# A Mamba and mixture-of-experts block on one core: the accumulating transfers of blocks 6 and 7 are sent first as a pair, those of blocks 0 to 5 after them

## The reference, cut to what matters

```python
x = L0_attn_x
xn = _layernorm(x, axis=-1)
x = x + _L0_attn_ref(xn, ...) + _L0_ffn_ref(xn, ...)
```

```python
top_logits, sel = jax.lax.top_k(logits, TOP_K)          # TOP_K = 2
probs = jax.nn.softmax(top_logits, axis=-1)
h = silu(einsum('td,edh->eth', xt, w1)) * einsum('td,edh->eth', xt, w3)
y = einsum('eth,ehd->etd', h, w2)
out = einsum('ktd,tk->td', y[sel.T, t_idx], probs)
```

## Time and profile before

| | us |
|---|---|
| median of 3 runs | 491.26 (490.94 to 491.74) |
| the profiled execution, whole time | 491.12 |
| its span, first to last instruction | 489.1 |
| DVE busy | 410.9 (84%) |
| PE busy | 436.3 (89%) |
| POOL busy | 319.8 (65%) |
| DMA queue of POOL | 25.52 MB, 19.6% of 16 engines' span |
| DMA queue of SP | 35.37 MB, 28.3% |

### The profile page before, as it was taken

The page is one execution under the profiler, slowest core; times in us unless marked ns, Lnnn a source line. Parts: engine busy times, 40 slices in busy tenths (PEclk is TensorE's granted clock), DMA queues, the critical chain, the costliest instruction groups (busy, mean ns, idle before and its releaser), DMA issues. The chain is left out here.

```text
span 489.1 us, 8269 instructions
## 1 busy us (share of the span) xinstructions
PE 436.3 (89%) x2188; PEld 318.8 (65%) x2188; DVE 410.9 (84%) x868; ACT 311.5 (64%) x421; POOL 319.8 (65%) x345
## 2 busy tenths in 40 slices
PE   0989959899999999998999999999999999996853
PEld 0887525555555555553788989888888999543432
DVE  5999986999999999996996777767776886894995
ACT  2775657888898888988544444343444555797650
POOL 3647778777787777680177777777777777755110
PEclk9999989999999999999999999999999999999975
DMA  9601139121121212132668776666665651049994
GB/s 246 176 3 46 56 105 168 52 75 63 50 87 49 89 45 84 39 114 57 175 190 231 225 210 181 193 184 180 176 183 160 184 170 60 7 79 204 211 194 129
DMA packets 70939, 62.75 MB, mean 128 GB/s; under 512 B 9034, under 2 KB 63214, under 8 KB 70912
## 3 DMA queue, kind: packets, MB, share of 16 engines
q1 hardware_dynamic: 57728, 35.37, 28.3%
q0 software_dynamic: 10944, 25.52, 19.6%
q10 hardware_dynamic: 2240, 1.57, 1.0%
HBM read 38.94 MB, written 29.64 MB: 140 GB/s over the span
## 5 line engine op out<-in xcount | busy, mean ns | idle before, releaser
L572 POOL DMA_INDIRECT moe_out<-xnT,dst_u x142 | 145.5, 1024 | 64.3 <-issue 31.7
L558 POOL DMA_INDIRECT moe_in<-xn,slot_u x128 | 141.6, 1106 | 46.1 <-issue 35.7
L1092 ACT ACTIVATE xn<-PA 128x1024 f32<-128x1024 f32 (+1 forms) x36 | 36.6, 1017 | 61.3 <-PE PA L803 52.7
L1447 DVE TENSOR_TENSOR xn<-xn,PB 128x1024 f32<-128x1024 f32 (+1 forms) x36 | 43.4, 1206 | 33.2 <-PE PB L803 29.2
L837 PE MATMUL PD<-xnT,xn 128*128 128x128 f32 x536 | 65.7, 275 | 0.0
L837 PEld LDWEIGHTS PD<-xnT,xn 128*128 128x128 f32 x536 | 62.8, 192 | 0.0
L1307 DVE SCALAR_TENSOR_TENSOR acc<-PA,cw,acc 128x255 f32<-128x255 f32 (+2 forms) x96 | 54.3, 607 | 8.2 <-ACT acc L1001 8.0
L685 PE MATMUL PC<-xc,Wc 128*128 128x512 f32 x128 | 57.7, 593 | 1.8 <-ACT xc L1048 1.8
L658 PE MATMUL PD<-xc,WgB 128*128 128x512 f32 x128 | 58.5, 601 | 0.0
L658 PEld LDWEIGHTS PD<-xc,WgB 128*128 128x128 f32 x128 | 24.8, 195 | 31.3 <-issue 31.3
L672 PE MATMUL PB<-WoT,y 128*128 128x128 f32 x240 | 32.2, 290 | 13.2 <-DVE y L1283 13.2
(11 more groups left out here) (211 smaller groups left out, 936.0 us busy)
## 6 DMA issues: line engine op xcount, KB each, us to landing
xnT<-in_L_ffn_w_dram SPq DMA_DIRECT2D x108, 128.0 KB, 2.3
xn<-moe_in SPq DMA_DIRECT2D x31, 266.0 KB
out_dram<-moe_out POOLq DMA_DIRECT2D x10, 512.0 KB, 10.2
out_dram<-xacc SPq DMA_DIRECT2D x7, 512.0 KB, 3.5
xacc<-moe_out POOLq DMA_DIRECT2D x6, 512.0 KB, 9.8
moe_out<-xnT,dst_u POOLq DMA_INDIRECT x142, 2.8
moe_in<-zrow SPq DMA_DIRECT2D x8, 266.0 KB, 6.6
moe_in<-xn,slot_u POOLq DMA_INDIRECT x128, 2.4
```

The lines of the kernel that those rows point to most:

```text
L558: gp.indirect_dma_start(xs_dram, bass.IndirectOffsetOnAxis(ap=slot_u[:, k, j:j + 1], axis=0), xn_row[:, j, :], None).then_inc(s_scat, 16)
L572: gp.indirect_dma_start(yt_dram, bass.IndirectOffsetOnAxis(ap=dst_u[:, t, j:j + 1], axis=0), yo[t % OUTS][:, j, :], None, bounds_check=PAI ...
L1092: act.activation(halves(sil, t), halves(PA[:, :], t), ACT.Silu).then_inc(s_sil, 1)
L1447: ve.tensor_tensor(halves(hid[b], t), halves(sil, t), halves(PB[:, :], t), ALU.mult).then_inc(s_hid, 1)
```

## The change

One line: the tuple of two groups of four blocks becomes one group of two and one of six.

```diff
-SUMS = ((6, 7, 0, 1), (2, 3, 4, 5))
+SUMS = ((6, 7), (0, 1, 2, 3, 4, 5))
```

## The result

The changed kernel takes 489.42 us at the median of 6 runs (488.94 to 490.05), the kernel before 491.59 in the runs beside them; the ratio is 0.9957, with an interval from 0.9945 to 0.997. It is faster by 2.1 us. The forecast was 486.8, a gain of 4.5 us, and its range ended at 489.1, so the result lies 0.3 us outside it: right in direction, half in size. In a second comparison of the same two (the experiment after_rounds) the ratio was 0.9957 again (0.9942 to 0.9973).

A forecast was written before the change was run, and what follows sets the result against it. It took DVE as the bound after step 14, held up by 6.2 queued behind three transfers. 6.2 4.85 us earlier, less 0.35 for SP's stores, gains 4.5: span 484.6, plus 2.02 is 486.6, 486.8 as median; range 485.6 to 489.1.

The forecast's parts named there:

- The head of the queue: Transfer 6.2, issued at 439.00 behind 7.1 alone, lands at 444.2 instead of 449.05, 4.85 us earlier (4.4 to 5.25).
- The covers on DVE, PE and ACT: From step 14 on, other engines' work is ready in time, so all shifts with DVE; a lost cover costs 0.85 us.
- The stream: POOL's transfers keep their pace after the reorder, so the last, 5.2, lands at 477.1 as before (476.1 to 477.9).
- the thirteen landings behind 6.2: Transfers from 7.2 to 5.2 follow at 2.48 us each, 32.2 us, to 476.4, or at 2.56 each to 477.5.
- a short queue is not slow by itself, an empty one is: DMA queue at the head: 61 and 74 GB/s at the empty start, against 205 with one transfer left at 474.
- The tail: SP's stores behind 5.2's landing end the span 7.5 us later, at 484.6, 0.35 us after DVE's side.
- Rival 1: Transfers behind 6.2 take 2.67 to 2.69 us each, 5.2 lands at 478.6 to 479.5, time 488.6; chance 0.16.
- the port rule: POOL's issues: certain vector instructions lock GpSimd out of the shared port, so issues beside a busy DVE would be long.
- Rival 2: A queue six deep lengthens every transfer; slower from 2.98 us each, 495.1 us at 3.2 each; chance 0.06.
- A slow two-deep phase: Head of the queue: named as making the forecast wrong, transfers not running at 2.5 us each with two in flight.
- DVE's side: End by DVE's last addition (481.95) and its small store: span ends at 484.25, ends 484.0 to 484.7.

The follow-up runs named there:

- order4_flight2: Kernel before, same order of transfers, but with two in flight at most; first to last landing 47.0 us against 38.5.
- paced4: Changed kernel with a wait before each issue, so that four transfers at most are in flight; 489.92 us, ratio 0.9958 to the kernel before.
- all_first: Changed kernel with one group of eight, all first rows issued before all second rows; 502.4 us, first to last landing 38.4 us.
- four_first: Changed kernel with block 4 ahead of 0 to 3 in the second group; disturbed chip, so only its stream is used, 40.8 us.
- order4_flight3: Kernel before, same order of transfers, but with three in flight at most; first to last landing 38.8 us.
- base_again: Kernel before profiled once more, no edit; first to last landing 38.5 us, span ended at 488.7.
- three_flight: Changed kernel with block 0 moved into the first group (6, 7, 0, then 1 to 5); 489.86 us, ratio 0.996 to the kernel before.
- filler: Changed kernel with 0.1 and 1.1 issued between 6.2 and 7.2; 564.0 us on a disturbed chip (ratio 1.0021), 488.78 us (0.9934) when repeated.
- pairs: Changed kernel with groups of two throughout: (6,7), (0,1), (2,3), (4,5); 495.9 us, first to last landing 47.9 us.
- again: Changed kernel profiled once more, no edit; first to last landing 41.5 us.
- five_early_sp: Changed kernel with block 5 ahead of 0 to 4 and POOL's last wait, for blocks 0 to 4, given to SP; 487.27 us, ratio 0.9903.
- five_early: Changed kernel with block 5 ahead of 0 to 4 in the second group; 488.79 us, ratio 0.9943 to the kernel before.

## Why the prediction was half right

**The head of the queue: right.** 6.2 landed at 444.6 (forecast 444.2, ends 443.8 and 444.64), which is the end that charged a whole start. DVE's wait went from 6.36 to 1.84 us, and PE's for L703 is gone:

```profile
444.66 0.69 DVE L1319 TENSOR_TENSOR xacc<-PB,xacc 128x512 f32<-128x512 f32 x1 [1.84 <-DMA xacc<-moe_out]
...
445.83 1.88 PE L703 MATMUL PB<-xnT,WinT 128*128 128x512 f32 x4
```

**The covers on DVE, PE and ACT: right.** L1044 came at 451.71 (453.1 at the latest, and less if PE's clock stayed up, which it did: over L703 the granted clock was 1.00, its upper level of 2.4 GHz, and 0.70 on the mean in the kernel before), softplus at 452.49 (452.1), and the shift of 4.5 us reached DVE's last addition whole: 482.33 against a forecast of 481.95.

```profile
451.71 1.02 ACT L1044 ACTIVATE thg<-PD 128x1024 f32<-128x1024 f32 x1
452.49 1.38 DVE L1293 SCALAR_TENSOR_TENSOR ebuf<-PC,nbdt,ebuf 128x512 f32<-128x512 f32 x2
```

**The stream: wrong, and the step that failed.** The sum kept 5.2 at 477.1, with 477.9 as the far end; it landed at 479.6. The term that was mis-sized is the thirteen landings behind 6.2: 32.2 to 33.3 us at 2.48 to 2.56 each in the prediction, 35.05 in the trace (444.56 to 479.61), 2.70 each. Two inferences carried it. One was to give all later transfers the spacing of the full queue. The other was the sentence that "a short queue is not slow by itself, an empty one is", drawn from the 205 GB/s of 474 to 475 us. There one transfer is left and drains; nothing new is issued behind it. What the change does is another thing: it issues a transfer with one ahead of it. order4_flight2 prices that at 0.6 us each. The trace of before had no row of it, so it had to be bounded, not excluded, and a bound was at hand: 6.1's 5.64 us from issue to landing. The prediction used it as the far end for 6.2 and not at all for 7.2, which landed 5.37 us after its issue at 441.72.

Against fifteen spacings of 2.48 us (37.2) this stream loses 3.9. From the first to the fourth landing, with the two issued into the short queue, it loses 1.1 (8.55 us where three full spacings are 7.44; the kernel before loses 0.4 there). 7.2 to 0.1 took 4.59 us, 2.1 too many, of which 1.8 is one thing: the sixteen engines no longer finish together. In the records of 0.1 twelve of its sixteen steps stand within 0.6 us and the last four 1.4 to 2.0 us behind the middle; in those of 7.2 all stand within 0.4 us. A transfer has landed when its slowest engine is done, and in a full queue each engine needs about the same 2.48 us for each transfer, so most of a lag stays to the end (1.3 us at 5.2, where it is 0.9 in the kernel before). That the engines finish independently and the semaphore counts them is what the Trainium skill says on the page "DMA: Bandwidth & Descriptors", section "Why a DMA increments its semaphore by 16 and not by 1". The slow ninth transfer adds 0.6 (3.08 us from 3.1 to 4.1). The kernel before loses 1.3 by the same count, above all 0.3 at 1.1 and 0.8 at 1.2, and the difference is the 2.6.

A part of the lag has nothing to do with the order. In both kernels one engine also carries a fetch of instructions in the midst of the stream, 16 KB in one packet: at 453.76 for 0.98 us in the kernel before, just ahead of 1.2's late landing, and at 449.87 for 1.00 us in the change, between the steps of 0.1. What the order costs is therefore better read by the middle engine: 40.0 us in the change and 37.9 before, 2.1 of the 2.6. There the loss stands at 6.2, 7.2 and 0.1 (3.20, 2.78 and 2.75 us), at 1.1 (3.11) and at 4.1 (2.95), and the other 0.5 us is the slowest engine's lag.

**What is open.** Why the stream stays slow for some transfers after the queue is full, in 446 to 451 and 458 to 462 us. Windows of before (first) and of the change (second) in the same stretches:

```profile
447.00:452.00 5.00, 2.03 (x4) 1.01 (x5) 2.86 (x5) 3.65 (x4) 4.64 (x5) 0.91 1.06 209
...
458.00:462.00 4.00, 3.10 (x7) 1.44 (x8) 3.93 (x5) 3.95 (x6) 0.83 (x1) 1.00 1.06 210
```

```profile
447.00:452.00 5.00, 4.15 (x10) 1.52 (x8) 5.00 (x9) 4.91 (x6) 1.13 (x3) 1.00 1.00 178
...
458.00:462.00 4.00, 4.00 (x23) 2.81 (x22) 3.92 (x6) 2.51 (x4) 0.81 (x1) 1.00 1.06 185
```

It is not the depth (paced4, all_first), not block 4 (four_first), and it is absent where the start had three or four equal issues and went on at that depth (before, order4_flight3). That it follows from the short queue at the head is only argued. By the middle engine the streams stand in that order: 37.9 us where three or more stood ahead of each issue behind the start (before, base_again, all_first), 38.3 and 38.6 with two (order4_flight3, three_flight), 39.1 in filler and filler_b, where one was issued with a single one ahead, 39.1 to 40.0 in the executions with the change's head, 45.9 and 47.9 in order4_flight2 and pairs. But four_first, with the change's head, has 39.1 like the fillers, and no run says how a transfer that is issued into a full queue still comes to be slow.

**The tail: right.** From 5.2's landing to the end of the span were forecast 7.5 us; 7.4 in the profiled execution, in again and in after_rounds. That the stores would be late next was seen too; but with the stream 2.5 us later they cost 2.5 us more. The whole miss of the span, 487.0 for 484.6, is the stream's.

**The rivals.** Rival 1, a later stream, had nearly the right outcome (488.6, 5.2 at 478.6 to 479.5) by luck and the wrong cause. Its 2.69 us were not the spacing of a deep queue: of those four landings three stand 2.49 to 2.51 us apart and one, 1.2's, 3.27, which is the late engine of the fetch; for the same reason the widest spacing was not 2.77. Issues of up to 3.15 us did come, and all_first had them too, with the shortest stream; so the port rule that was weighed there did not decide anything here. It is a rule for certain kinds of vector instructions, so that it makes no issue long for a busy DVE alone, and the 2.67 us of 5.1 are the end of a row of issues sent back to back (0.81, 1.12, 1.43, 1.75, 2.67), no sign of it. Rival 2, the deep queue, is refuted by paced4 and all_first. A slow two-deep phase, named among what would make the forecast wrong, was what came at the head, and had neither price nor chance of its own. The range left it out. (In the prediction's ends, DVE's side begins at 489.1 - 5.25 = 483.85 and not 484.0; nothing hangs on it.)

## What to carry to other kernels

Moving a wanted transfer forward is worth what the chain of waits says, here 4.5 us on DVE's side. But a full queue serves at the best rate, and an order that leaves two in flight gives that rate up, 0.6 us for each issue in order4_flight2; the price turns up at the end of the stream, so look who waits for its last transfer before the gain is booked. And each path to the end has a tail of its own, here SP's stores (7.4 us), POOL's wait with its drain (6.3 us) and DVE's last addition with its store (2.3 us): taking away the longest brings the next. Of the kernels that compute the whole output, the gain came whole only in five_early_sp, where neither the stores nor POOL's drain hung on the last landing.

## What the runs showed of the hardware

- A transfer of 512 KB added from DRAM takes 2.48 us in an undisturbed full queue (211 GB/s); fifteen took 38.4 to 38.8 us in four executions with three or more always in flight, 39.8 in a fifth (three_flight, with one late engine; 38.6 by the middle one). With two it is 3.1 us on the mean of order4_flight2 (47.0 / 15). The engines' busy share does not show the loss.
- Once the sixteen engines have drifted apart in a full queue they mostly stay so: 0.87 to 0.88 us over the last nine landings of the kernel before. It is no law: in after_rounds the slowest engine was 1.2 us behind the middle one at 0.1 and 0.5 at 1.1, and in order4_flight2 a lag of 1.5 us at 0.2 was 0.1 two transfers later.
- POOL's closing drain takes 5.79 us when it starts behind POOL's wait for blocks 0 to 4, in all kernels here that have this wait but order4_flight2 (5.94), and ended 2.9 us behind the last landing when it was started early.
- Stores of another queue beside such a stream take 14.3 to 15.0 us in place of 3.3 to 4.7 (five_early), and slow the stream from 2.48 to 2.8 us a transfer; the packets of the two queues go one for one.
- One fetch of instructions, 16 KB on one DMA engine for 0.98 us, set that engine 0.9 us behind for the rest of the stream in the kernel before: from 1.2 on its step stands 0.9 us behind the middle one. In base_again the fetch came at 462.26 and the lag, 1.0 us, begins at 4.1.
